# A back chunk's four steps between attention and the output projection, spread to one per key tile

## The chip, the core and the metric
The kernel runs on one core of a Trainium2 chip. The metric is device time in microseconds, the median of several executions. In the profile, TensorE is PE (its weight loads PEld), VectorE DVE, ScalarE ACT, GpSimd POOL, and SyncE, which here only issues transfers, SP (its queue SPq).

## What is computed
The reference is one block of a transformer with a feed-forward part on either side of attention, in fp32, on an input x of 2 x 1024 tokens by 512:

```python
x = x + 0.5 * ffn(layernorm(x))
x = x + attention(layernorm(x))
x = x + 0.5 * ffn(layernorm(x))
```

ffn is a 512 x 512 linear layer with a bias, plus a low-rank part of rank 16 from 8 experts, of which the two best by a router count for a token. attention has 32 heads of 16 dimensions over 8 key and value heads; its four projections multiply with the signs of the weights and scale each output column. Softmax divides by the sum of the exponentials. The kernel does this division late: it leaves attention with unnormalised outputs and the sums beside them, and the change is about the place at which outputs are multiplied with the inverted sums.

## The kernel before, in words
Tokens are worked in chunks of 256. A front chunk goes through the first feed-forward part and the Q, K, V projections; a back chunk takes the attention outputs through the output projection, the residual sum and the second feed-forward part. The first six front chunks are worked before attention begins.

Attention has 32 units: 4 blocks of 512 queries times 8 key heads. A unit goes through 8 key tiles of 128 keys. In a key tile TensorE makes four score products (one for each query head that shares the key head), ScalarE four exponentials of them, and TensorE the products with V of the tile before (line 1516: four instructions, each of which stands as two records). Beside this, TensorE makes the maximum products of the unit after next (line 1485), two uses of a two-bank PSUM tile to a key tile, and VectorE reduces each (line 1312, 1.2 us each) to a negative maximum. In each unit's second key tile TensorE turns the shifts once (line 1494) and VectorE copies them out (line 1321); in its first, ScalarE copies the unit's output to SBUF (line 1027).

The attention loop is written as eight bodies of 4 units, 32 key tiles (`slot` 0 to 31) each. Bodies 0 and 1 carry the last two front chunks as filler work, bodies 2 to 7 the six back chunks 1 to 6 in the numbering of this text. The last two back chunks come after attention (the tail), interleaved with a lag of 7 lines.

The filler's order is a list of lines, `BACK`. Line k belongs to key tile k/2. Each engine's loop over key tiles picks its own share of a line, at these places:

```python
# TensorE: scores 0, 1; products with V; [turn]; scores 2, 3; max pair 0; line 2*slot; max pair 1; line 2*slot + 1
# ScalarE: exp 0, 1; line 2*slot - 1; exp 2, 3; [copy of the output]; line 2*slot
# VectorE: line 2*slot - 1; [copy of the shifts]; reduce pair 0; line 2*slot; reduce pair 1
```

Every engine works in its own program order. A wait in a filler step therefore holds all that is behind it on that engine: on VectorE the reductions, on ScalarE the third exponential of the tile.

TensorE's scores 0 and 1 of a tile need exponentials 2 and 3 of the tile before (two PSUM banks), its products with V need exponential 3 of the tile before, its maximum products need the reduction two uses back.

The steps at issue, for a back chunk:
- NR (line 8 of the list; `invert_sums`, code line 1162): VectorE inverts the sums. SyncE then stores them to DRAM (552).
- NL (line 9; `load_recip`, 563): when the store is complete, SyncE issues four loads that bring them back, each row to the 16 partitions of its head.
- N0a, N0b: for the first and the second 128 tokens, VectorE waits for the outputs and for all four loads and multiplies (1252); ScalarE then casts the product to the high part for the projection (953).
- N0al, N0bl: VectorE subtracts the high part from the product (1258), which is the low part.
- Oa0, Oa1, Ob0, Ob1: TensorE's projection (1470), four products a piece; Oa0 waits for N0al, Ob0 for N0bl. VectorE scales the result (1304) at Oa1 and Ob1.
- C0, C1, G0, G1, P0, P1: clamps and guards; ADD: the residual sum.

In the tail the sums of the last head group come straight from SBUF, and N0a first inverts those (1250).

Of the kernel before, what the change touches and what calls it, by code (L numbers as in the profile page):

```python
# [49 lines left out]
BACK = [s.split() for s in (  # L50
    8 * [""] + ["NR", "NL", "", "", "", "", "", "N0a", "N0al N0b", "N0bl", "", "Oa0", "Oa1", "C0", "Ob0", "Ob1", "", "G0 C1", "P0", "", "G1", "P1",
    "ADD", "", "LN1a", "LN1b", "", "LN1c", "LN1d", "T1a", "T1al", "", "T1b", "T1bl", "", "RT", "", "RU",
    "R0", "R1", "R2 HT0", "R3 R4 HT1", "R5", "", "WR", "", "WH FFa0", "WL FFa1", "FFa2", "FFa3 FFa4", "",
    "FFb0", "FFb1", "FFb2", "FFb3 FFb4"])]
# [1552 lines left out]
```

## Time and profile before

| | us |
|---|---|
| median of 3 executions | 1164.65 (1163.46 to 1167.42) |
| the profiled execution's own time | 1162.77 |
| its span, first to last instruction | 1161.0 |
| TensorE busy | 1061.4 (91%) |
| VectorE busy | 837.9 (72%) |
| ScalarE busy | 727.0 (63%) |
| POOL busy | 295.4 (25%) |

Busy times are sums over the whole span. What a step costs has to be read from the stretch it stands in: there, at which engine the others wait last. The mean granted clock of TensorE over the span is 0.959 of 2.4 GHz.

### The profile page before, as it was taken

Reading aid. Unit: us, or ns where it says so; the run is one execution under the profiler, and the core shown is the slowest. Engines: PE = TensorE matmul, PEld = TensorE weight load, DVE = VectorE, ACT = ScalarE, POOL = GpSimd, SP = SyncE. Lnnn points to the kernel's source line nnn. Section 1 sums busy time; section 2 is a strip of 40 time slices with the busy share of each in tenths; the row PEclk is TensorE's granted clock in tenths of the full one; section 3 lists DMA queues with packets and bytes.
Section 4 is the critical chain, followed back from the end, with each engine's and each line's share of the span. In section 5 each row is a group of like instructions: output and inputs, shape, how many; then the busy total and the mean of one; then the engine's idle time right before and its main releaser. Section 6 shows DMA issues by size and latency. Waiting matters only on the chain.

```text
span 1161.0 us, 16018 instructions
## 1 busy us (share of the span) xinstructions
PE 1061.4 (91%) x5776; PEld 466.8 (40%) x5776; DVE 837.9 (72%) x1107; ACT 727.0 (63%) x1361; POOL 295.4 (25%) x485
## 2 busy tenths in 40 slices
PE   5989887999999999999999999999999999999647
PEld 4778661344334422333334333433343334233236
DVE  5766679767777777876787778777877887871274
ACT  6556432757865786675676667666767675768311
POOL 5355546302420240410050023003200420041010
PEclk9989886999999999999999999999999999999869
DMA  7122331021211123111211121121113010301300
GB/s 254 46 81 88 100 103 49 27 73 36 60 49 35 33 59 105 31 32 48 87 31 31 61 75 31 31 87 48 31 31 110 30 40 17 115 10 33 108 0 37
DMA packets 70507, 68.31 MB, mean 59 GB/s; under 512 B 15132, under 2 KB 52508, under 8 KB 70428
## 3 DMA queue, kind: packets, MB, share of 16 engines
q1 hardware_dynamic: 70428, 67.29, 18.9%
q8 instruction: 46, 0.75, 0.3%
q14 instruction: 33, 0.27, 0.1%
HBM read 41.95 MB, written 24.63 MB: 57 GB/s over the span
## 4 chain that ended last, share of the span: by engine, by line
PE 72%; DVE 13%; ACT 5%; DMA 3%; issue 3%; POOL 3%; SPq 1%; DVEq 0%; ACTq 0%; POOLq 0%
PE ps_out L1516 19%; PE ps_score L1504 18%; PE ps_max L1485 16%; PE ps_fill L1441 5%; DVE neg_max L1312 5%; ACT probs L1018 2%; PE ps_fill L1470 2%; PE ps_fill L1423 2%; PE ps_fill L1445 1%; DVE neg_max L1110 1%; DVE zd L1184 1%; PE ps_out L1441 1%; PE ps_fill L1409 1%; PE ps_fill L1415 1%; DVE xn L1252 1%
## 5 line engine op out<-in xcount | busy, mean ns | idle before, releaser
L1018 ACT ACTIVATE probs<-ps_score 128x512 f32<-128x512 f32 x992 | 539.0, 597 | 262.0 <-PE ps_score L1504 260.9
L1312 DVE TENSOR_REDUCE neg_max<-ps_max 128x1 f32<-128x1024 f32 x480 | 570.9, 1219 | 179.7 <-PE ps_max L1485 177.7
L1504 PE MATMUL ps_score<-qst,kst 99*128 99x512 bf16 x992 | 308.9, 387 | 10.1 <-ACT probs L1018 8.5
L1485 PE MATMUL ps_max<-kst,qst 96*128 96x512 bf16 x1024 | 290.1, 389 | 16.8 <-DVE neg_max L1110 5.8
L1516 PE MATMUL ps_out<-probs,v_ring 128*32 128x512 f32 x2048 | 274.7, 608 | 7.3 <-ACT o_sb L1027 4.9
L1504 PEld LDWEIGHTS ps_score<-qst,kst 99*128 99x128 bf16 x992 | 76.0, 97 | 273.6 <-ACT probs L1018 232.4
L1485 PEld LDWEIGHTS ps_max<-kst,qst 96*128 96x128 bf16 x1024 | 91.4, 99 | 144.5 <-issue 19.5
L852 POOL CAST shift<-neg_max 128x16 bf16<-128x16 f32 x32 | 9.2, 286 | 435.0 <-DVE neg_max L1312 430.6
L1516 PEld LDWEIGHTS ps_out<-probs,v_ring 128*32 128x32 f32 x2048 | 40.9, 108 | 95.6 <-issue 87.2
L948 ACT ACTIVATE xn<-xc,ln_shift,rstd 128x512 f32<-128x512 f32 x48 | 38.6, 814 | 30.6 <-POOL ln_shift L748 19.6
L1441 PE MATMUL ps_fill<-wb_h,xt_h 128*128 128x512 f32 x84 | 47.1, 561 | 1.0 <-DVE xc L1299 0.8
L769 POOL TENSOR_TENSOR xc<-xc,bias_half 128x512 f32<-128x512 f32 x28 | 36.6, 1332 | 28.0 <-ACT xn L948 27.4
L1110 DVE TENSOR_REDUCE neg_max<-ps_max 128x1 f32<-128x1024 f32 x32 | 37.6, 1215 | 3.9 <-PE ps_max L1485 3.5
L780 POOL TENSOR_SCALAR zd<-zm 128x512 f32<-128x512 f32 x12 | 23.0, 1919 | 64.1 <-DVE zm L1304 64.1
L1470 PE MATMUL ps_fill<-so,xt_h 128*128 128x512 f32 x56 | 28.1, 501 | 12.0 <-DVE xt_l L1258 11.3
L1441 PE MATMUL ps_fill<-wb_h,xt_l 128*128 128x512 f32 x84 | 34.0, 405 | 0.0
L1441 PE MATMUL ps_fill<-wb_l,xt_h 128*128 128x512 f32 x84 | 34.0, 405 | 0.0
L780 POOL TENSOR_SCALAR zm<-zd 128x512 f32<-128x512 f32 x12 | 23.0, 1920 | 41.6 <-ACT zd L984 34.2
L743 POOL TENSOR_SCALAR var_eps<-meanvar 128x2 f32<-128x2 f32 x18 | 4.9, 270 | 101.8 <-DVE meanvar L1234 96.2
L837 POOL TENSOR_TENSOR zm<-zd,zm 128x512 bf16<-128x512 f32 (+1 forms) x24 | 24.8, 1062 | 20.6 <-ACT zm L1012 20.6
L1299 DVE SCALAR_TENSOR_TENSOR xc<-ps_fill,xc 128x512 f32<-128x512 f32 x21 | 14.5, 691 | 20.7 <-PE ps_fill L1445 20.7
L837 POOL TENSOR_TENSOR zd<-zd,zm 128x512 f32<-128x512 f32 (+1 forms) x24 | 23.7, 1017 | 22.2 <-ACT zm L1009 22.2
(254 smaller groups left out, 1296.6 us busy)
## 6 DMA issues: line engine op xcount, KB each, us to landing
qst<-q_dram SPq DMA_DIRECT2D x192, 64.0 KB, 2.2
att_dram<-o_sb SPq DMA_DIRECT2D x31, 256.0 KB, 2.1
q_dram<-zm SPq DMA_DIRECT2D x24, 256.0 KB, 2.6
kst<-k_dram SPq DMA_DIRECT2D x192, 32.0 KB, 2.2
xc<-x SPq DMA_DIRECT2D x8, 512.0 KB, 4.0
x_dram<-xc SPq DMA_DIRECT2D x8, 512.0 KB, 2.9
xc<-x_dram SPq DMA_DIRECT2D x8, 512.0 KB, 5.6
out<-xc SPq DMA_DIRECT2D x8, 512.0 KB, 3.1
```

Source lines behind the costliest of these rows:

```text
L769: gp.tensor_tensor(xc[s][:, t, :], xc[s][:, t, :], bias_half[:, :], ALU.add).then_inc(bias_added[s], 1)
L780: gp.tensor_scalar(upper[:, cols], value[:, cols], 0.0, BIG, ALU.max, ALU.min).then_inc(clamped[s], 1)
L837: last = gp.tensor_tensor(rest, kq[:, piece], parts[s][:, k - 1, piece], ALU.subtract)
L948: act.activation(xn[s][:, t, :], xc[s][:, t, :], ACT.Identity, bias=ln_shift[s][:, t:t + 1], scale=rstd[s][:, t:t + 1]).then_inc(xn_ready[ ...
L1018: act.activation(probs[:, kt % 2, j, :], score_bank(i, uu, j), ACT.Exp, scale=1.0 / HD ** 0.5).then_inc(probs_ready, 1)
L1110: dve.tensor_reduce(neg_max[:, v, t:t + 1], ps_max[use % 2][:, :, :], AXY, ALU.max, negate=True).then_inc(max_read, 1)
L1312: dve.tensor_reduce(neg_max[:, uu % 2, t:t + 1], ps_max[max_slot(uu, pos)][:, :, :], AXY, ALU.max, negate=True).then_inc(max_read, 1)
L1441: pe.matmul(ps[:, :], x_part[s][:, c, tok], w[:, c, :], start=(c == 0 and k == 0), stop=False)
L1470: last = pe.matmul(ps[:, :], x_part[s][:, c, tok], so[:, c, :], start=(c == 0 and x_part is xt_h), stop=(c == DC - 1 and x_part is xt_l))
L1485: last = pe.matmul(ps_max[slot][:, half, :], qst[0:SR, r, j, q * P:(q + 1) * P], kst[0:SR, r, half * 512:half * 512 + 512], start=True, st ...
L1504: pe.matmul(score_bank(i, uu, j), kst[0:SR + PARTS, uu, kt * P:(kt + 1) * P], qst[0:SR + PARTS, uu, j, :], start=True, stop=True).then_inc ...
L1516: last = pe.matmul(ps_out[32 * j:32 * j + 32, :], v_ring[:, k, kt, :], probs[:, kt % 2, j, :], start=(kt == 0), stop=(kt == KT - 1))
```

## The change
The four steps are spread. No instruction is added or removed.

```diff
 BACK = [s.split() for s in (
-    8 * [""] + ["NR", "NL", "", "", "", "", "", "N0a", "N0al N0b", "N0bl", "", "Oa0", "Oa1", "C0", "Ob0", "Ob1", "", "G0 C1", "P0", "", "G1", "P1",
+    8 * [""] + ["NR", "NL", "", "", "", "N0a", "", "N0al", "", "N0b", "", "N0bl Oa0", "Oa1", "C0", "Ob0", "Ob1", "", "G0 C1", "P0", "", "G1", "P1",
```

Counted from line 0 of the list:

| step | line before | line after | key tile before | key tile after |
|---|---|---|---|---|
| NR, NL | 8, 9 | 8, 9 | 4, 5 | 4, 5 |
| N0a | 15 | 13 | 8 | 7 |
| N0al | 16 | 15 | 8 | 8 |
| N0b | 16 | 17 | 8 | 9 |
| N0bl | 17 | 19 | 9 | 10 |
| Oa0 | 19 | 19 | 9 (its end) | 9 (its end) |

Steps on an odd line come between exponentials 1 and 2 on ScalarE and ahead of the reductions on VectorE; on an even line, after exponential 3 and between the two reductions. In the tail, VectorE's order for the two chunks A and B changes from ... Oa1(A), C0(A), N0a(B), Ob1(A), N0al(B), N0b(B), N0bl(B), G0(A), C1(A), P0(A), Oa1(B) ... to ... Oa1(A), N0a(B), C0(A), N0al(B), Ob1(A), N0b(B), G0(A), C1(A), P0(A), N0bl(B), Oa1(B) ...

## Rows read from the trace of the kernel before

**Rows 1.** The page's chain that ended last, by line.
```profile
PE ps_out L1516 19%; PE ps_score L1504 18%; PE ps_max L1485 16%; PE ps_fill L1441 5%; DVE neg_max L1312 5%; ACT probs L1018 2%; PE ps_fill L1470 2%; PE ps_fill L1423 2%; PE ps_fill L1445 1%; DVE neg_max L1110 1%; DVE zd L1184 1%; PE ps_out L1441 1%; PE ps_fill L1409 1%; PE ps_fill L1415 1%; DVE xn L1252 1%
```
**Rows 2.** Timeline, TensorE, chunk 3 (start, us, engine, line, instruction, idle before).
```profile
674.50 1.06 PE L1516 MATMUL ps_out<-probs,v_ring 128*32 128x512 f32 x8
...
677.38 1.07 PE L1516 MATMUL ps_out<-probs,v_ring 128*32 128x512 f32 x8
...
680.73 0.88 PE L1504 MATMUL ps_score<-qst,kst 99*128 99x512 bf16 x2 [0.88 <-ACT probs L1018]
681.80 1.07 PE L1516 MATMUL ps_out<-probs,v_ring 128*32 128x512 f32 x8 [0.19 <-ACT o_sb L1027]
```
**Rows 3.** Windows: engines' busy us; last PEclk, DMA share, GB/s.
```profile
676.50:677.00 0.50, 0.50 (x4) 0.10 (x1) 0.43 (x1) 0.50 (x2) 0.00 (x0) 1.00 0.02 6
897.00:897.50 0.50, 0.50 (x7) 0.26 (x4) 0.50 (x1) 0.11 (x1) 0.00 (x0) 1.00 0.02 6
1010.00:1010.50 0.50, 0.50 (x8) 0.00 (x0) 0.50 (x2) 0.50 (x2) 0.00 (x0) 1.00 0.08 27
...
569.94:575.40 5.46, 5.46 (x22) 2.00 (x22) 3.97 (x6) 2.80 (x6) 0.00 (x0) 0.69 0.16 54
681.80:686.14 4.34, 4.18 (x22) 1.63 (x22) 3.64 (x6) 2.79 (x6) 0.00 (x0) 1.00 0.29 89
```
**Rows 4.** Chain in order of time, chunks 1 and 2 (start, us, what).
```profile
443.95 4.59 DMA recip_dram<-sums
...
450.45 3.92 DMA zd<-recip_dram
...
461.67 0.93 PE ps_fill L1470 x4
...
562.67 4.22 DMA zd<-recip_dram
```
**Rows 5.** Timeline, ScalarE, chunk 3.
```profile
675.92 1.08 ACT L1018 ACTIVATE probs<-ps_score 128x512 f32<-128x512 f32 x2 [0.50 <-PE ps_score L1504]
...
679.56 0.63 ACT L953 ACTIVATE xt_h<-xn 128x512 fp32r<-128x512 f32 x1 [1.26 <-DVE xn L1252]
680.10 1.07 ACT L1018 ACTIVATE probs<-ps_score 128x512 f32<-128x512 f32 x2
```
**Rows 6.** Timeline, VectorE, chunk 3.
```profile
673.69 2.36 DVE L1312 TENSOR_REDUCE neg_max<-ps_max 128x1 f32<-128x1024 f32 x2 [0.62 <-PE ps_max L1485]
676.57 2.36 DVE L1312 TENSOR_REDUCE neg_max<-ps_max 128x1 f32<-128x1024 f32 x2 [0.53 <-PE ps_max L1485]
678.85 0.68 DVE L1252 TENSOR_TENSOR xn<-xn,zd 128x512 f32<-128x512 f32 x1
```
**Rows 7.** Timeline, VectorE, reductions of key tile 6 in chunks 1, 2, 4, 5, 6.
```profile
448.10 2.36 DVE L1312 TENSOR_REDUCE neg_max<-ps_max 128x1 f32<-128x1024 f32 x2 [0.62 <-PE ps_max L1485]
...
561.27 2.36 DVE L1312 TENSOR_REDUCE neg_max<-ps_max 128x1 f32<-128x1024 f32 x2 [0.63 <-PE ps_max L1485]
...
784.42 2.36 DVE L1312 TENSOR_REDUCE neg_max<-ps_max 128x1 f32<-128x1024 f32 x2 [0.62 <-PE ps_max L1485]
...
895.15 2.36 DVE L1312 TENSOR_REDUCE neg_max<-ps_max 128x1 f32<-128x1024 f32 x2 [0.62 <-PE ps_max L1485]
...
1005.90 2.36 DVE L1312 TENSOR_REDUCE neg_max<-ps_max 128x1 f32<-128x1024 f32 x2 [0.62 <-PE ps_max L1485]
```
**Rows 8.** Timeline, SyncE's queue: the four loads of chunks 3, 4 and 6.
```profile
671.95 2.47 SPq L563 DMA_DIRECT2D zd<-recip_dram  x4
...
783.09 2.47 SPq L563 DMA_DIRECT2D zd<-recip_dram  x4
...
1005.53 2.47 SPq L563 DMA_DIRECT2D zd<-recip_dram  x4
```
**Rows 9.** Timeline, TensorE, key tile 9's scores in chunk 2.
```profile
568.88 0.88 PE L1504 MATMUL ps_score<-qst,kst 99*128 99x512 bf16 x2 [1.44 <-ACT probs L1018]
```
**Rows 10.** Timeline, VectorE, the tail.
```profile
1109.58 0.69 DVE L1258 TENSOR_TENSOR xt_l<-xn,xt_h 128x512 fp32r<-128x512 f32 x1 [0.70 <-ACT xt_h L953]
```

## The prediction
> **What bounds the kernel now.** I read the page's chain of waits by line first [rows 1]: it is led by TensorE's three kinds of attention product, none of which the change touches. So the question is where the four steps that it moves hold TensorE. They stand in six loop bodies (back chunks 1 to 6 below, one in each) and once more for the two tail chunks. I then read one body, that of back chunk 3, engine by engine.
>
> TensorE [rows 2]: the products with V of successive key tiles start at 674.50, 677.38, 681.80 and (the end of the stretch in [rows 3]) 686.14. The first distance, 2.88 us, is a key tile with nothing between. The next is 4.42, so key tile 8, in which the old line 15 falls, loses 4.42 - 2.88 = 1.54; its row shows 0.88 idle until the exponentials came. The third, 4.34, has 0.93 of projection in it (four products [rows 4]); 4.34 - 2.88 - 0.93 = 0.53 is left for the turn of the shifts and for exponentials that came late. A back chunk's four steps thus cost about 1.54 plus part of 0.53.
>
> ScalarE [rows 5] says why. Between the second and third exponential of a key tile it does the cast of line 15. In tile 7 it had 0.50 of idle at that place; in tile 8 it stood 1.26 until VectorE had made the product, then cast, and the third exponential began at 680.10. VectorE [rows 6] says why the product was late: reductions of the tile before fill it (2.36 in 2.88), and they end after ScalarE has asked. The reductions of tile 6 end at 673.69 + 2.36 = 676.05; ScalarE was ready for the third exponential of tile 7 at 675.92 - 0.50 = 675.42. VectorE is 0.63 behind one tile earlier too. Its lag isn't made by the four steps, and it does not go with them.
>
> The product needs the inverted sums back from DRAM. In chunks 1 and 2 [rows 4] the chain that ended last runs through that round trip: the store took 4.59 until it was seen (chunk 1), and the last of the four loads 3.92 and 4.22, landing at 450.45 + 3.92 = 454.37 and 562.67 + 4.22 = 566.89. The product of line 15 already waited for it there.
>
> **The change part by part.** No operation is added or removed; NR and NL, and so SyncE's queue and the requests at lines 8 and 9, stay. Products, casts and subtractions move.
>
> *N0a from line 15 to 13* is one key tile earlier: from ahead of VectorE's reductions of tile 8 to ahead of those of tile 7. (a) With the reciprocals in place the stall is the same one: VectorE's lag is the same, the product and cast take as long, so 1.54 moves from tile 8 to tile 7. I cost that at nothing. (b) The reciprocals are asked for 2.88 earlier. VectorE is free after tile 6, by its rows, at [rows 6, 7]: 450.46, 563.63, 676.05, 786.78, 897.51 and 1008.26. In chunks 1 and 2 it waited before, so a whole tile more: 2 x 2.88 = 5.8. For chunk 3 the last load was requested one request (0.6) before its row's end [rows 8], 671.95 + 2.47 - 0.6 = 673.8, and the transfer share is down to 0.02 in 676.5 to 677.0 [rows 3]; I take 676.9, 3.1 after the request, so a wait of 0.9. Chunk 4: request at 785.0, by the same 3.1 landing at 788.1, wait 1.3. Chunk 5: the share is 0.02 already from 897.0, so none. Chunk 6: request 1007.4, share 0.08 in 1010.0 to 1010.5, landing 1010.5, wait 2.3. Sum: 5.8 + 0.9 + 1.3 + 0 + 2.3 = 10.3. From both sides: had all landed at the earliest moment that shares allow, 676.5, 787.9, 897.0 and 1010.0, it is 5.8 + 0.5 + 1.1 + 0 + 1.7 = 9.1; with the 4.22 of chunk 2 everywhere, 5.8 + 2.0 + 2.4 + 1.2 + 3.4 = 14.8. I keep 10.3, since the shares are these chunks' own. Queued behind VectorE's wait are the reductions of tile 7; for them wait TensorE's maximum products and POOL's split of the shifts; ScalarE waits for the product with its third exponential, and TensorE with the next tile's scores. No slack stands on that ring (tiles follow each other at 2.88 with TensorE full), so I count each wait in full.
>
> A rule speaks against this. The Trainium skill (DMA: Bandwidth & Descriptors, "Anatomy of one DMA") puts a DMA's fixed cost at about 2.0 us, size aside. By it store, requests and loads would be through in 2.0 + 1.9 + 2.0 and a little, near 450.1 in chunk 1, and nobody would wait: the sum without (b) and the clock. The rows of chunk 1, 4.59 and 3.92, do not agree here, where other transfers are under way.
>
> *The clock.* In chunk 2 TensorE idled 1.44 in tile 8 [rows 9], and the stretch behind it ran at a mean granted clock of 0.69, part of it at the lower level, 1.2 GHz; in chunk 3 it idled 0.88 and the clock stayed at 1.00, 2.4 GHz. The same stretch took 5.46 and 4.34 [rows 3]: a fall costs 1.12. With the waits above chunks 3, 4 and 6 idle 0.88 + 0.9, + 1.3 and + 2.3, all over 1.44: three new falls, 3.4. Chunks 1 and 2 have theirs already. Bounds: none, 0; in all six one more, 6.7. I take three, the rows on either side of 1.44 being this clear.
>
> *N0al from 16 to 15, N0b from 16 to 17, N0bl from 17 to 19.* N0b's cast leaves the end of tile 8, where it pushed the exponentials of tile 9, for the middle of tile 9. The product comes after tile 8's reductions, so ScalarE waits for it as in tile 7, some 1.3 less the 0.5 it idles anyway: 0.8. But tile 9 ends with four projection products, 0.93 of TensorE's time [rows 4], which cover it; uncovered it would be 6 x 0.8 = 4.8 more. What goes is the late exponentials' part of 0.53; I take 0.3 of it, for the turn stays: 6 x -0.3 = -1.8, at best 6 x -0.53 = -3.2. N0al and N0bl go ahead of the reductions of tiles 8 and 10; projection piece Oa0 needs N0al alone, and N0bl is due at Ob0, two tiles on. Nothing for both. The projection itself stays at line 19.
>
> *The tail* has the same list without attention around it. The second chunk's product moves ahead of the first's clamps, and its last low part behind the first's guard. So the 0.70 in which VectorE stood for a cast [rows 10] is filled: -0.7, at worst 0, since VectorE is busy from there to the first chunk's statistics.
>
> **Sum:** 10.3 + 3.4 - 1.8 - 0.7 = +11.2 on the profiled execution's 1162.77, 1174.0. The median of the runs shown is 1.9 above that execution; I add half of it: 1175.
>
> **The rivals.**
> *A, faster:* the four steps bunched in one and a half tiles are what holds ScalarE, and one to a tile fits. Then the 1.54 goes in all six chunks, with it the two falls of clock, and the 1.8 and 0.7: 9.2 + 2.2 + 1.8 + 0.7 = 13.9, about 1149. It decides if VectorE has N0a's product ready when ScalarE asks in tile 7. For it speaks that VectorE does 4.4 us of work in tile 8 (three times 0.68, and 2.36); against it that ScalarE's long wait comes before the first of them, behind reductions alone [rows 5, 6]. 4 in 100.
> *B, the reciprocals are there in time* (what the page's rule above gives): no wait and no fall, -1.8 - 0.7 = -2.5, about 1161, on the edge of what can be told. Against it stand the two landings in the chain [rows 4]. 7 in 100, half of them faster.
> *C, the waits are taken up* in slack that I don't see, by half or more: 10.3 and 3.4 shrink to under 6, and with -2.5 it ends at 1163 to 1168. 6 in 100.
> *D, much slower:* N0b's wait in tile 9 isn't covered by the projection: the -1.8 becomes +4.8, about 1182. It decides if VectorE ends tile 8's reductions over 0.9 late. 10 in 100.
> The forecast has 73 in 100; its own range is 1168 to 1181.
>
> **How the numbers follow.** Three tenths of a per cent, 3.5 us, is about what a measurement can tell from no change: faster is under 1161.2, slower over 1168.1. Faster: A 4 and half of B, 7 in 100. Same: the rest of B and C, 10. Slower: forecast and D, 83. The range 1164 to 1182 leaves out A, most of B, half of D and the ends of the forecast, about 2 in 10.
>
> **What would show it.** Right: in tile 7 of each body VectorE's product N0a stands behind idle time put down to the loads of the reciprocals, about 3.9 in chunk 1, 3.3 in chunk 2, 0.9, 1.3, none, 2.3; the distance of products with V is over 4.4 between tiles 7 and 8 and 2.88 plus the copy of the output between 8 and 9; clock falls behind five of six; no ScalarE wait for N0b that TensorE shows. Wrong: the loads land before 676 in chunk 3, or the waits stand there and the bodies are no longer; ScalarE's cast in tile 7 without idle before it (A); TensorE idle in tile 10 until exponentials (D).

## The result, and the profile after

The changed kernel took 1181.38 us (median of 4, 1175.34 to 1187.41) against 1164.06 before: ratio 1.0148, interval 1.0089 to 1.0208. Run once more later it gave 1179.44, ratio 1.0126 (1.0098 to 1.0155). It is slower by 15 to 17 us, 1.3 to 1.5 per cent, clear of no change. (One of the later runs' executions, with x1's load moved, took 1493.93 at a mean granted clock of 0.651 and is left out of its ratio.) The profiled execution took 1175.34, 12.6 more than that of before. It had been 4.2 faster by the start of body 2, ahead of all that the change touches: the products with V of that body begin at 427.28 in the changed kernel and at 431.45 in the one before. From there to the end it is 16.7 slower: 18.0 in the six bodies (first to last product with V, 673.3 against 655.3) less 1.3 in the tail (72.9 against 74.2 behind the last such product).

The page's engine totals and chain after. The first two lines answer to the table of before, the third to [rows 1]:

```profile
span 1173.5 us, 16018 instructions
PE 1063.9 (91%) x5776; PEld 462.8 (39%) x5776; DVE 838.5 (71%) x1107; ACT 727.0 (62%) x1361; POOL 296.9 (25%) x485
PE ps_out L1516 19%; PE ps_score L1504 17%; PE ps_max L1485 15%; PE ps_fill L1441 4%; DVE neg_max L1312 4%; PE ps_fill L1470 2%; ACT probs L1018 2%; DMA zd<-recip_dram 2%; DMA recip_dram<-sums 2%; PE ps_fill L1423 1%; PE ps_fill L1445 1%; PE ps_out L1441 1%; DVE neg_max L1110 1%; DVE zd L1184 1%; PE ps_fill L1409 1%
```

No engine has more to do. What is new is in the chain: the store of the reciprocals and their loads, 2% each. Before, VectorE's products N0a waited for the loads in chunks 1 and 2 alone, 1.6 in all (start, us, engine, line, instruction, idle before):

```profile
454.47 0.77 DVE L1252 TENSOR_TENSOR xn<-xn,zd 128x512 f32<-128x512 f32 x1 [1.13 <-DMA zd<-recip_dram]
...
566.98 0.69 DVE L1252 TENSOR_TENSOR xn<-xn,zd 128x512 f32<-128x512 f32 x1 [0.47 <-DMA zd<-recip_dram]
```

After, they wait in all six bodies:

```profile
450.96 0.69 DVE L1252 TENSOR_TENSOR xn<-xn,zd 128x512 f32<-128x512 f32 x1 [4.68 <-DMA zd<-recip_dram]
...
564.16 0.69 DVE L1252 TENSOR_TENSOR xn<-xn,zd 128x512 f32<-128x512 f32 x1 [1.37 <-DMA zd<-recip_dram]
...
680.66 0.69 DVE L1252 TENSOR_TENSOR xn<-xn,zd 128x512 f32<-128x512 f32 x1 [2.13 <-DMA zd<-recip_dram]
...
794.63 0.69 DVE L1252 TENSOR_TENSOR xn<-xn,zd 128x512 f32<-128x512 f32 x1 [1.41 <-DMA zd<-recip_dram]
...
907.40 0.69 DVE L1252 TENSOR_TENSOR xn<-xn,zd 128x512 f32<-128x512 f32 x1 [0.82 <-DMA zd<-recip_dram]
...
1020.95 0.69 DVE L1252 TENSOR_TENSOR xn<-xn,zd 128x512 f32<-128x512 f32 x1 [1.47 <-DMA zd<-recip_dram]
```

The sum is 11.9. Now TensorE in chunk 5, the one with the shortest wait; it answers to [rows 2]:

```profile
905.04 1.06 PE L1516 MATMUL ps_out<-probs,v_ring 128*32 128x512 f32 x8
...
909.39 0.79 PE L1504 MATMUL ps_score<-qst,kst 99*128 99x512 bf16 x2 [1.88 <-ACT probs L1018]
910.11 1.82 PE L1516 MATMUL ps_out<-probs,v_ring 128*32 128x512 f32 x8
```

ScalarE and VectorE ahead of it, answering to [rows 5] and [rows 6]:

```profile
908.13 0.63 ACT L953 ACTIVATE xt_h<-xn 128x512 fp32r<-128x512 f32 x1 [2.17 <-DVE xn L1252]
```

```profile
904.23 2.36 DVE L1312 TENSOR_REDUCE neg_max<-ps_max 128x1 f32<-128x1024 f32 x2 [0.62 <-PE ps_max L1485]
907.40 0.69 DVE L1252 TENSOR_TENSOR xn<-xn,zd 128x512 f32<-128x512 f32 x1 [0.82 <-DMA zd<-recip_dram]
```

VectorE is free at 904.23 + 2.36 = 906.59 and stands until the loads have landed; ScalarE, which asked earlier, stands 2.17 in place of 1.26. TensorE's idle time has gone from 0.88 to 1.88, and the products with V behind it take 1.82 in place of 1.07. The windows between the starts of successive products with V show why. Their columns are as in [rows 3]: length, then the busy times of PE, PEld, DVE, ACT and POOL, then the granted clock, the DMA share and GB/s. Tile 7 to 8, 8 to 9, 9 to 10:

```profile
905.04:910.11 5.07, 3.17 (x18) 0.85 (x17) 4.25 (x5) 2.83 (x6) 0.00 (x0) 1.00 0.38 113
910.11:914.58 4.47, 4.47 (x18) 1.08 (x17) 1.65 (x3) 2.46 (x6) 1.52 (x5) 0.62 0.25 67
914.58:918.83 4.25, 4.13 (x22) 1.50 (x21) 4.25 (x6) 2.68 (x6) 0.00 (x0) 1.00 0.18 65
```

In the middle one TensorE is busy all the time and at a mean clock of 0.62, part at 1.2 GHz. The same three distances in every chunk (tiles 7 to 8, 8 to 9, 9 to 10):

| chunk | before | after |
|---|---|---|
| 1 | 2.88, 5.71, 5.47 | 9.16, 4.23, 4.02 |
| 2 | 2.88, 4.97, 5.46 | 5.84, 5.39, 5.39 |
| 3 | 2.88, 4.42, 4.34 | 6.61, 5.14, 3.85 |
| 4 | 2.88, 4.41, 4.34 | 5.66, 4.48, 4.12 |
| 5 | 2.88, 4.42, 4.34 | 5.07, 4.47, 4.25 |
| 6 | 2.88, 4.41, 4.35 | 5.94, 4.23, 4.05 |

The mean clock of tile 8 to 9 is 0.71, 0.50, 0.53, 0.62, 0.62 and 0.71 after, so it fell in all six chunks; before it was 1.00 there, and fell in chunks 1 and 2 a tile later (0.69). From tile 10 on the bodies are alike again.

### The profile page after: what moved, and what is told of

Read it like the earlier page. It is cut to its first block, busy times and chain, and to the rows that moved or that the text cites. A ratio compares the mean times of both kernels' runs of the same rounds, so it can differ in the third digit from the quotient of the medians.

```text
span 1173.5 us, 16018 instructions
## 1 busy us (share of the span) xinstructions
PE 1063.9 (91%) x5776; PEld 462.8 (39%) x5776; DVE 838.5 (71%) x1107; ACT 727.0 (62%) x1361; POOL 296.9 (25%) x485
## 4 chain that ended last, share of the span: by engine, by line
PE 70%; DVE 13%; ACT 5%; DMA 4%; issue 3%; POOL 3%; SPq 2%; DVEq 0%; ACTq 0%; POOLq 0%
PE ps_out L1516 19%; PE ps_score L1504 17%; PE ps_max L1485 15%; PE ps_fill L1441 4%; DVE neg_max L1312 4%; PE ps_fill L1470 2%; ACT probs L1018 2%; DMA zd<-recip_dram 2%; DMA recip_dram<-sums 2%; PE ps_fill L1423 1%; PE ps_fill L1445 1%; PE ps_out L1441 1%; DVE neg_max L1110 1%; DVE zd L1184 1%; PE ps_fill L1409 1%
## 5 line engine op out<-in xcount | busy, mean ns | idle before, releaser
L1485 PE MATMUL ps_max<-kst,qst 96*128 96x512 bf16 x1024 | 291.3, 390 | 16.8 <-DVE neg_max L1110 5.5
L1516 PE MATMUL ps_out<-probs,v_ring 128*32 128x512 f32 x2048 | 279.3, 618 | 6.6 <-ACT o_sb L1027 4.1
L953 ACT ACTIVATE xt_h<-xn 128x512 fp32r<-128x512 f32 x16 | 10.1, 630 | 44.2 <-DVE xn L1252 44.2
```

Source lines behind the costliest of these rows:

```text
L1485: last = pe.matmul(ps_max[slot][:, half, :], qst[0:SR, r, j, q * P:(q + 1) * P], kst[0:SR, r, half * 512:half * 512 + 512], start=True, st ...
L1516: last = pe.matmul(ps_out[32 * j:32 * j + 32, :], v_ring[:, k, kt, :], probs[:, kt % 2, j, :], start=(kt == 0), stop=(kt == KT - 1))
```

## The experiments

The theory: three things happened. VectorE waits for the reciprocals a tile earlier; the idle time that this makes on TensorE brings its clock down, which costs once more; and the spreading of the other steps is a small gain. The rival: the spreading is itself the loss. Each ratio below is to the kernel before, run beside it, with its 95% interval. The diffs show the part of the list's line that differs from the kernel before, unless they say otherwise.

**Only the later steps spread.**

```diff
-"N0a", "N0al N0b", "N0bl", "", "Oa0",
+"N0a", "N0al", "N0b", "", "N0bl Oa0",
```

> N0a stays at line 15 (tile 8); only N0b goes from 16 to 17 and N0bl from 17 to 19 (N0al stays at 16). My theory (the loss is the earlier wait for the reciprocals and the clock that falls behind it; the rest of the change is a small gain): the distance between tiles 9 and 10 falls from 4.34 to about 4.04 in every chunk, 1.8 in all, and the tail gives about 1: some 3 us under the kernel before. Rival (the spreading itself costs, since ScalarE now waits 1.1 for N0b in the middle of tile 9): 4 to 6 us over it.

Measured: 1158.32, ratio 0.9958 (0.9944 to 0.9972), 5 us faster than before. TensorE in chunk 3:

```profile
674.23 1.06 PE L1516 MATMUL ps_out<-probs,v_ring 128*32 128x512 f32 x8
677.57 0.88 PE L1504 MATMUL ps_score<-qst,kst 99*128 99x512 bf16 x2 [0.88 <-ACT probs L1018]
678.64 1.06 PE L1516 MATMUL ps_out<-probs,v_ring 128*32 128x512 f32 x8 [0.19 <-ACT o_sb L1027]
682.46 1.06 PE L1516 MATMUL ps_out<-probs,v_ring 128*32 128x512 f32 x8
```

Tiles 8 to 9 are 4.41 as before; 9 to 10 are 682.46 - 678.64 = 3.82 in place of 4.34. That is 0.5 for a chunk, more than the 0.3 I had: the whole of the remainder of 0.53 that the prediction read from [rows 3]. The tail did not change (74.0). In the profiled execution the six bodies are 2.6 shorter than before; the rest of the 5 us lies ahead of them or is not traced. The rival falls.

**Only N0a moved.**

```diff
-"", "", "", "", "", "N0a", "N0al N0b", "N0bl",
+"", "", "", "N0a", "", "", "N0al N0b", "N0bl",
```

> Only N0a goes to line 13; N0al, N0b at 16 and N0bl at 17 as before. My theory: all of the loss is here, so 17 to 22 us over the kernel before, with VectorE idle for the loads ahead of N0a in every chunk and the clock at 0.50 behind it. Rival (half the loss belongs to the spreading): 8 to 12 over it.

Measured: 1192.00, ratio 1.0240 (1.0209 to 1.0271), 29 over the kernel before and more than I expected. VectorE's waits for loads, in the list of who waited for whom (total, times, longest), are larger in this run:

```profile
DVE xn L1252 <- DMA zd<-recip_dram: 15.7, 6, 4.8
```

That is 3.8 more than after the full change. The distances of tiles 9 to 10 sum to 32.8 over six chunks against 25.7, 7 more. With N0al and N0b still bunched in tile 8, ScalarE waits there a second time, and TensorE idles again:

```profile
698.18 0.88 PE L1504 MATMUL ps_score<-qst,kst 99*128 99x512 bf16 x2 [1.17 <-ACT probs L1018]
```

So behind an early N0a, spreading the others is worth more than it is alone, about 7 in place of 3 in these profiles. The loss belongs to N0a.

**The changed order without the wait for the reciprocals.** In the loop's six chunks the attention outputs are multiplied by a resident tile, so this kernel leaves out the division by the softmax sums; the loads are still made and awaited at N0bl.

```diff
-                    dve.wait_ge(recip_loaded[ch.att], (ch.att_use + 1) * 16 * DC)
+                    if ch.tail:
+                        dve.wait_ge(recip_loaded[ch.att], (ch.att_use + 1) * 16 * DC)
...
-                    dve.tensor_tensor(att_t[ch.att][:, :, tok], att_t[ch.att][:, :, tok], recip_t[ch.att][:, :, tok],
+                    factor = recip_t[ch.att][:, :, tok] if ch.tail else o_scale[:, :].rearrange("p (c n) -> p c n", c=DC)
+                    dve.tensor_tensor(att_t[ch.att][:, :, tok], att_t[ch.att][:, :, tok], factor,
...
                     dve.wait_ge(xt_h_ready[s], ch.t0 + (t + 1))
+                    if t == 1 and not ch.tail:
+                        dve.wait_ge(recip_loaded[ch.att], (ch.att_use + 1) * 16 * DC)
```

> The changed kernel, but in the six back chunks of the loop N0a and N0b multiply by a resident tile (the output scale) and not by the loaded reciprocals, which are awaited at N0bl only: the division by the softmax sums is left out there. My theory: no wait for loads at line 13; the stall by VectorE's lag stays (products with V 4.4 apart between tiles 7 and 8), TensorE idles about 0.9, the clock doesn't fall. Kernel before minus its own two waits (1.6), its two falls (2.3), minus 1.8 and minus 1.3: 7 us under the kernel before, about 1157. Rival (the place in tile 7 is bad in itself): at or over the kernel before, 1164 to 1170.

**The same edit in the order of before.**

> The kernel before with the same edit (the division left out in the six chunks of the loop). My theory: its waits of 1.1 and 0.5 in chunks 1 and 2 go, and the two falls of clock that cost 1.1 each: 3 to 4 us under the kernel before, all six chunks alike at 4.42 and 4.34. Rival (waiting for loads costs nothing beyond VectorE's lag): no difference.

Measured: 1157.81 (0.9949, 0.9932 to 0.9966) in the changed order and 1159.55 (0.9972, 0.9962 to 0.9982) in the old one. TensorE in chunk 3 of the first:

```profile
672.05 1.07 PE L1520 MATMUL ps_out<-probs,v_ring 128*32 128x512 f32 x8
675.49 0.79 PE L1508 MATMUL ps_score<-qst,kst 99*128 99x512 bf16 x2 [0.97 <-ACT probs L1018]
676.21 1.06 PE L1520 MATMUL ps_out<-probs,v_ring 128*32 128x512 f32 x8
679.35 1.07 PE L1520 MATMUL ps_out<-probs,v_ring 128*32 128x512 f32 x8 [0.19 <-ACT o_sb L1027]
683.32 1.06 PE L1520 MATMUL ps_out<-probs,v_ring 128*32 128x512 f32 x8
```

All six chunks are alike within 0.03: 4.16, 3.14, 3.98 in the changed order, 2.88, 4.41, 4.34 in the old. This pair is the ruler for the rest. Without waiting for loads the change gains 0.35 a chunk. The stall by VectorE's lag is the same in tile 7 as in tile 8, 4.16 - 2.88 = 1.28, and the copy of the output adds 0.26 where it stands. ScalarE waits twice now, 1.25 for N0a and 1.08 for N0b, and the second wait leaves no idle row on TensorE: the projection covers it.

**x1's load moved from tile 4 to tile 11**, in the changed kernel. x1 is the chunk's residual, used at ADD, line 30 of the list. Why is the round trip late? In chunk 1 of the kernel before, the 512 KB load of x1 goes out 1.5 us ahead of the store (timeline, SyncE's queue):

```profile
442.48 0.45 SPq L526 DMA_DIRECT2D xc<-x_dram  x1
...
443.95 0.34 SPq L552 DMA_DIRECT2D recip_dram<-sums  x1
```

Over the six chunks it is 1.5, 2.1, 3.1, 3.7, 3.4 and 2.2 ahead, and the store takes 4.6, 3.6, 2.4, 2.8, 1.6 and 3.8 until it lands: in the main, the closer the load, the later the store.

```diff
-                    if slot == 4 and load_next is not None:
+                    if slot == 11 and load_next is not None:
                         load_x1(load_next, chunk_loaded[0])
```

> The changed kernel with the 512 KB load of the residual (x1) asked for in key tile 11 and not in tile 4, where it runs beside the store of the reciprocals. My theory (the reciprocals come late because their store and loads share the engines with other transfers): the store is seen in 2 us or so in place of 2 to 4.5, so VectorE's six waits ahead of N0a shrink from 11.9 to under 4 in all; with them the falls of clock in the chunks without a wait: 12 to 18 us under the changed kernel, 1163 to 1169. Rival (the round trip is a fixed cost of two transfers in a row): waits and time as in the changed kernel, near 1181.

Measured: 1161.07, ratio 0.9985 (0.9966 to 1.0003). That is 18 to 20 under the changed kernel's two medians, 16 to 19 by the ratios, and below the 1163 to 1169 that I expected. From issue of the store to its landing, by the view of its line, in the changed kernel and then here:

```profile
DMA to landing us min/median/max: 2.2/3.0/5.2
```

```profile
DMA to landing us min/median/max: 1.4/1.5/5.1
```

(The longest are the tail's two.) VectorE's idle time ahead of its products, here:

```profile
  DMA zd<-recip_dram: 1.5, 4
```

From 11.9 to 1.5, with five of six chunks keeping their clock. A fixed cost of the round trip is ruled out. So is an earlier store: in both runs SyncE issues it 4.96 ahead of tile 7's products with V.

**The same in the kernel before.**

> The kernel before with x1's load in tile 11. My theory (x1's load holds up the round trip of the reciprocals): no wait for the loads at line 15 and no fall of clock in any chunk, the loop's six chunks alike at 4.42 and 4.34: 3 to 5 us under the kernel before, near 1159, as with the division left out. Rival (the round trip was late for another reason, and the changed kernel gained from something else): no difference.

Measured: 1159.35, ratio 0.9966 (0.9950 to 0.9981), and the loop's six chunks 4.41 and 4.34 to within 0.02, as with the division left out. So that load also made the two waits of the kernel before.

**Dummy products in the idle time.** At the end of tile 7 TensorE gets six products of constants, in the changed kernel (its list gets KEEP at line 15).

```diff
+                if pos == "KEEP" and not ch.tail:
+                    bnk, reads = ch.bank("Oa")
+                    pe.wait_ge(filler_read[bnk], reads)
+                    for _ in range(6):
+                        pe.matmul(ps_fill[bnk][:, :], so[:, 0, 0:P], wb_h[:, 0, :], start=True, stop=True)
```

> The changed kernel plus six dummy products on TensorE (512 columns, constants) at the end of tile 7 of each loop chunk, in the idle time ahead of tile 8's scores; their result is overwritten. My theory (idle time over about 1.4 brings the clock down and that is a cost of its own): idle falls by 1.4; in the chunks with a short wait (4, 5, 6, perhaps 3) the clock stays at 1.00 and the distance of products with V between tiles 8 and 9 comes down from 4.2 to 5.1 to about 3.1: 4 to 8 us under the changed kernel, 1173 to 1177. Rival (the lower clock costs nothing, since other engines bound there): no gain, 1181 to 1184.

Measured: 1171.79, ratio 1.0089 (1.0054 to 1.0124). That is 8 to 10 under the changed kernel's medians but 4 to 7 by the ratios (1.0126 and 1.0148), whose intervals overlap with this one; what carries the argument is the trace, chunk by chunk. TensorE and VectorE in chunk 5, where the loads were even later than in the profile above, 1.28 against 0.82:

```profile
912.68 1.74 PE L1391 MATMUL ps_fill<-wb_h,so 128*128 128x512 f32 x6
915.38 0.79 PE L1509 MATMUL ps_score<-qst,kst 99*128 99x512 bf16 x2 [0.96 <-ACT probs L1018]
```

```profile
913.39 0.69 DVE L1252 TENSOR_TENSOR xn<-xn,zd 128x512 f32<-128x512 f32 x1 [1.28 <-DMA zd<-recip_dram]
```

```profile
916.09:919.24 3.15, 2.96 (x18) 0.88 (x18) 1.93 (x3) 2.51 (x6) 1.45 (x5) 1.00 0.29 90
```

Idle 0.96, the clock stays at 1.00, and tile 8 to 9 takes 3.15 as without any wait. In chunks 4, 5 and 6 the stretch from tile 7 to 11 less VectorE's wait is 15.16, 15.16, 15.17; in the changed kernel it is 16.64, 16.76, 16.53. The fall of clock thus costs about 1.5 beside the wait that brings it. With the clock held, tiles 8 to 10 take 7.13, as in the pair that doesn't wait (7.12): in these chunks nothing but the clock was lengthening them. In chunks 1, 2 and 3, with waits of 5.4, 3.0 and 3.2, six products are too few and the clock falls as before: there the low clock stays in the sum.

**The changed kernel again.**

> The changed kernel itself once more, for a second profile and beside the others on one chip. My theory: VectorE's six waits for the loads sum to 10 to 16 us and differ from run to run, and time follows their sum: 1175 to 1187, with a fall of clock behind every wait that leaves TensorE idle over 1.4. Rival (the loss is fixed, the landings only coincide): the time is the same to 0.3 per cent whatever the waits sum to.

Measured: 1179.44; the profiled execution took 1183.68, 8.3 more than the one above. Of that, 4.5 lie ahead of body 2, which the change doesn't touch, 3.6 in the six bodies (676.9) and 0.2 in the tail. The waits are 4.6, 4.1, 1.5, 0.9, 0.8 and 1.2, 13.0 in all, 1.1 more; 2.1 of the 3.6 stand in tiles 8 to 10 (55.7 against 53.6), where the low clock is. Chunk 3 here waited as long as chunk 6 above, 1.46 and 1.47. Windows of its tiles 8 to 9 and 9 to 10, and then those of chunk 6 above:

```profile
688.16:693.55 5.39, 5.39 (x17) 1.24 (x16) 2.22 (x4) 2.66 (x6) 1.51 (x5) 0.50 0.22 72
693.55:699.04 5.49, 5.49 (x23) 1.87 (x22) 3.28 (x5) 2.59 (x6) 0.00 (x0) 0.68 0.07 22
```

```profile
1023.87:1028.10 4.23, 4.05 (x17) 0.99 (x17) 1.64 (x3) 2.48 (x6) 1.52 (x5) 0.71 0.00 0
1028.10:1032.15 4.05, 4.02 (x22) 1.59 (x22) 3.99 (x6) 2.55 (x6) 0.00 (x0) 1.00 0.20 71
```

After the same wait the clock is at its lower level through the whole of tile 8 and a good part of tile 9 (means 0.50 and 0.68) in one case, and through part of tile 8 (0.71) in the other. The two tiles and the one ahead of them took 16.8 and 14.2, a difference of 2.6 for one chunk. Why it stayed low longer in one, these runs don't show. My expectation that time follows the sum of the waits was too simple.

**Cast half a tile behind its product.** If ScalarE's 1.28 comes from standing next to a VectorE that lags, the cast should be asked for later than the product. Products at 15 and 17, casts (H0a, H0b) at 16 and 18:

```diff
-"N0a", "N0al N0b", "N0bl", "", "Oa0",
+"N0a", "H0a", "N0al N0b", "H0b", "N0bl Oa0",
...
-                if pos in ("N0a", "N0b"):
+                if pos in ("H0a", "H0b"):
                     t = 0 if pos.endswith("a") else 1
                     act.wait_ge(att_normed[s], n * 2 + (t + 1))
```

> The kernel before with VectorE's products at lines 15 and 17 and ScalarE's casts each a line later, at 16 and 18; low parts at 17 and 19. My theory (the 1.54 per chunk is ScalarE waiting in front of its third exponential for a VectorE that lags by 0.6): the wait is gone, since VectorE has a half tile for the product; products with V 3.1 to 3.4 apart between tiles 8 and 9 in place of 4.42, no falls of clock: 9 to 12 us under the kernel before, 1151 to 1154. Rival (VectorE's three additions of 0.68 in tiles 8 and 9 are themselves the bound): the loss reappears as TensorE waiting for the reductions, 0 to 4 under the kernel before.

> The same with the load of x1 in tile 11. My theory: the waits for the loads at line 15 in chunks 1 and 2 (1.1 and 0.5) go too: 1 to 3 us under the one before. Rival: the load in tile 11 meets the loads of queries and keys and comes late for the residual sum: over it.

Measured: 1154.38, ratio 0.9936 (0.9913 to 0.9958), and with x1's load in tile 11 too 1151.84, ratio 0.9913 (0.9882 to 0.9943). Tile 8 to 9 is 3.15, but tile 9 to 10 is 4.59 in chunks 3 to 6 of the first run (5.85 and 5.64 in chunks 1 and 2, where N0a still waited 1.17 and 0.94 for loads) and in all six of the second. VectorE has two additions ahead of its copy of the shifts and its reductions there, and TensorE's second maximum pair waits for that copy:

```profile
676.17 0.60 PE L1485 MATMUL ps_max<-kst,qst 96*128 96x512 bf16 x2 [0.45 <-DVE shift_rows L1321]
```

So the rival was half right: the loss that is left is VectorE's.

**One addition to a tile, earlier and later.** Both with x1's load in tile 11.

```diff
+"", "", "", "", "N0a", "H0a", "N0b", "H0b N0al", "", "N0bl Oa0", "Oa1", "C0",
```

> Cast split from the product and x1's load in tile 11, as in the run of 1151.84, but one addition for VectorE to a tile: N0a at 14, cast 15, N0b at 16, cast 17, N0al at 17, N0bl at 19. My theory (tile 9 takes 4.59 there because both N0al and N0b stand ahead of its reductions, 1.4 in 2.9): tile 9 comes down to about 4.0, six times 0.6: 1147 to 1150. Rival (the place of N0a in tile 7 brings the wait for the loads back): VectorE waits at line 14 and the time is 1155 or over.

```diff
+"", "", "", "", "", "N0a", "H0a", "N0al", "N0b", "H0b Oa0", "Oa1", "N0bl C0",
```

> The same idea moved back: N0a 15, cast 16, N0al 17, N0b 18, cast 19, N0bl 21. My theory: the loads are never awaited; tile 9 about 4.0 to 4.2; but N0bl now stands with the scaling of Oa1 near tile 10 and 11 and may be late for Ob0: 1147 to 1153. Rival (VectorE is full in tiles 10 and 11): TensorE waits for N0bl ahead of Ob0, over 1153.

Measured: 1154.30 (0.9925, 0.9905 to 0.9944) and 1150.43 (0.9891, 0.9867 to 0.9914). The first expected 1147 to 1150 and missed: tile 9 to 10 stays at 4.60. From N0a (670.52 in chunk 3) on VectorE's rows follow each other there without a pause, and TensorE's maximum products wait for its reductions (0.17 and 0.29); that N0a in tile 7 leaves no time to catch up is my reading of it. The second has 2.88, 3.14, 3.98 in all six chunks, the shortest of all; its N0bl stands later, and tile 11 to 12 is 4.91 in place of 4.74. TensorE in its chunk 3, and ScalarE, whose cast no longer waits:

```profile
670.72 1.06 PE L1516 MATMUL ps_out<-probs,v_ring 128*32 128x512 f32 x8
...
673.86 1.07 PE L1516 MATMUL ps_out<-probs,v_ring 128*32 128x512 f32 x8 [0.19 <-ACT o_sb L1027]
...
677.85 1.06 PE L1516 MATMUL ps_out<-probs,v_ring 128*32 128x512 f32 x8
```

```profile
673.59 0.64 ACT L953 ACTIVATE xt_h<-xn 128x512 fp32r<-128x512 f32 x1
```

It beats the kernel before by 1.1 per cent, with the whole computation in place.

## Why the prediction was right, and where it was off

The direction, the place and the mechanism were right, and the time lies within the range of 1164 to 1182, near its upper end: +11.2 was forecast, +16.7 is in the profile from body 2 on. The median of 1181.38 is just above the forecast's own 1168 to 1181 and beside rival D's 1182, without D's mechanism. That the profiled execution took 1175.34 where 1175 was forecast is luck: it had been 4.2 faster before the change could act.

*The wait for the reciprocals, +10.3.* Measured 11.9 less the old 1.6: 10.3. The agreement is of the sum, and in part luck. By chunk it was 3.9, 3.3, 0.9, 1.3, 0, 2.3 forecast and 4.7, 1.4, 2.1, 1.4, 0.8, 1.5 found, and the other profiles with N0a at that place gave 13.0 (the changed kernel again) and 14.6 (with the dummy products). The single landings move by a microsecond or two from run to run; I had read one execution's as if they were fixed. The wait counted in full: nothing took it up (rival C), and the reciprocals were not there in time (rival B).

*N0a's own stall, nothing.* Right: 1.28 in tile 7 without loads to wait for, as in tile 8, with the copy's 0.26 left in tile 8. Rival A fell there. VectorE's lag is behind reductions alone; moving the cast to a later place took ScalarE's wait away.

*The clock, +3.4.* This is the term that failed. Set against the pair without waits, tiles 8 to 10 hold 53.6 in six chunks where 42.7 would do: 10.9 for the low clock. Before, all that is over the pair's old order is 4.1, less 1.6 of waits: 2.5. The change is +8.4. I had three things wrong. Chunk 5 was to keep its clock since its loads would be there in time; they were 0.8 late and it fell too, so that all six fell: 1.6 where I had none. I took 1.12 for a fall from tile 9 of chunk 2 alone; in tile 8 a fall costs 1.1 to 2.3 (3.14 without one), and chunks 3, 4 and 6 lost 4.5 where I had 3.4. And chunks 1 and 2 "have theirs already" was wrong for chunk 2, whose fall came a tile earlier and cost 2.3 in tile 8 and another 1.4 in tile 9, 2.4 more than before. That every idle time over 1.44 brought a fall here was in part luck: the first experiment has one of 2.46 without a fall (last section). The upper bound that I gave, 6.7, was below what happened.

*N0b and N0bl, -1.8.* Measured -0.35 a chunk, -2.1, from the pair; alone, in the old place, 0.5 a chunk. ScalarE's second wait was 1.08, where I had 1.3 (0.8 beyond the 0.5 that it idles anyway), and the projection covered it. Rival D didn't happen: TensorE has no idle row over 0.3 from tile 9 to 11 of any chunk.

*The tail, -0.7.* Measured -1.3. The idle of [rows 10] is gone; the other 0.6 I have not traced.

Sum: in tile 7 the six chunks take 38.3, 13.3 over the pair's 25.0, of which 11.9 are the waits. Of the 1.4 left, 0.3 stand in each of chunks 1, 2, 3 and 6, whose clock is below 1.00 in that stretch already (means 0.76 to 0.92), and 0.1 in each of the other two: most of it is the clock again. 13.3 + 10.9 - 4.1 - 2.1 - 1.3 = 16.7.

The Trainium skill (DMA: Bandwidth & Descriptors, "Anatomy of one DMA") put a DMA's fixed cost at about 2.0. Its figure is for transfers that GpSimd issues, and those here are SyncE's. With the 512 KB load out of its way the store landed in 1.5 (median), below that figure; beside that load it was 3.0. The loads took longer than it: with x1's load moved, in the four chunks where N0a still waited, the last one landed 3.1 to 3.5 behind its request, and the whole round trip took 6.7 to 7.3, where the prediction made about 6 of the rule. So by these runs it is short even for the round trip with that load out of the way.

## What to carry to other kernels

When a step that waits for a transfer is moved forward in a queue, price the wait by the landing and what is queued behind it, and look for the transfer that it shares the engines with: here moving one large load that nobody needed soon took 16 to 20 us back. A handoff between two engines that each work in program order wants its two ends a little apart: here half a key tile (1.44) was enough for a VectorE that lags by 0.63 and a product of 0.68. And where TensorE's clock falls behind an idle stretch, add a second price to the idle time itself: here 1.1 to 3.7 for each fall.

## What the runs showed that I had not expected

No run shows TensorE's clock fall in tile 8 behind an idle time of 1.36 or less, and it fell behind most from 1.44 up. But the idle time alone doesn't decide it. With only the later steps spread, TensorE idled 2.46 in tile 8 of chunk 1 (N0a waited 1.49 for the loads there), and the clock stayed at 1.00 through the two windows from tile 8 to 10:

```profile
454.95 0.88 PE L1504 MATMUL ps_score<-qst,kst 99*128 99x512 bf16 x2 [2.46 <-ACT probs L1018]
```

```profile
450.02:456.02 6.00, 3.25 (x18) 0.89 (x17) 4.51 (x6) 3.16 (x7) 1.06 (x5) 1.00 0.51 120
456.02:459.86 3.84, 3.84 (x22) 1.59 (x22) 3.12 (x5) 2.54 (x6) 0.00 (x0) 1.00 0.20 73
```

In the same chunk of the kernel before it fell behind 2.18. With only N0a moved, a second idle time of 1.62 in tile 9 of chunk 1 brought no fall either. What else decides it, these runs leave open.

How long the clock stays low varies behind the same wait of VectorE: means of 0.50 and 0.68 over two tiles of 5.4 and 5.5 us in one case, 0.71 over one tile of 4.2 us in the other. Filling the idle time with 1.7 us of products whose result nobody reads made the kernel faster by 4 to 10 us, on intervals that overlap. And a 32 KB store beside a 512 KB load took twice as long until it landed, 3.0 against 1.5.
